# A selective-scan layer with its MLP on one core: accumulating DMAs chained over three states instead of two

## The chip, the core and the metric

The kernel runs on 1 core of a Trainium2 chip. The metric is the device time of one execution in microseconds (us). Engines are named as in the profile: PE is TensorE (PEld its weight loads), DVE is VectorE, ACT is ScalarE, POOL is GpSimd, SP is SyncE. "The clock" is the granted clock of TensorE, as a share of 2.4 GHz.

## What is computed

The input x has 4 batches of 4096 positions with 512 channels, all in float32. The layer is an adaptive layer norm, a selective scan with 16 states per channel, a gated output projection with residual and layer norm, and then a small per-channel MLP. Cut to what matters here:

```
h = layernorm(x) * (1 + ca) + sa
x_ssm, z = split(h @ w_in.T + b_in);  z = silu(z)
dt = softplus(x_ssm @ w_dt.T + b_dt)
Bm = x_ssm @ w_B.T + b_B;  Cm = x_ssm @ w_C.T + b_C
A = -exp(A_log)
def step(state, inp):                      # over the positions
    xt, dtt, bt, ct = inp
    dA = exp(A[None] * dtt[..., None])
    dB = dtt[..., None] * bt[:, None, :]
    state = dA * state + dB * xt[..., None]
    y = sum(state * ct[:, None, :], axis=-1)     # over the 16 states
y = (y + D * x_ssm) * z
x = x + ga * (layernorm(y @ w_out.T + b_out + h) * gamma + beta)
h = layernorm(x) * (1 + cb) + sb
x = x + gb * ffn(h)                        # 512 -> 64, relu of 16 each, -> 512
```

The change concerns the sum over the 16 states in the line that begins with `y = sum`.

## The kernel before

**Tiling.** The positions are cut into 32 chunks of 512, worked through one after another. In a chunk the channels stand on the partitions, in KD = 4 blocks of 128, and the scan runs along the 512 positions. A **unit** is one state of one channel block, so a chunk has 64 units: unit i is state i // 4, block i % 4. I call one pass over the 64 units a **step**, and position i in it **slot** i. In step s the scan of chunk s runs; beside it the dense work of the next chunk (norm, projections, dt, u: the tensors xs_t, dt_t, u_t) and of the two chunks before (output projection, second norm, MLP).

**One unit's way.** ACT makes the decay (L842) and, per state, the input v (L852). PE turns v into channel-major form in PSUM (`turn_v`, L524; the instruction's own line is L468, b_ps). The transpose for unit i + 1 stands at the start of slot i and waits until scan i - 1 is done. DVE scans (L1140, into `hs`, a ring of 6 units). POOL multiplies two units at once with C (L379, the product, into `pr`, a ring of 10 units). PE adds the product into y_ps by four transposes (`add_unit`, L533, instructions L543). Scan i needs product i - 6 to be done. A product needs its place in `pr` free: the unit ten before must have been added by PE, or copied on by a DMA.

**Chained states.** States in HELD are not added by PE. Once the next state's product is made, POOL issues a DMA (`add_products`, L387) that adds the held product into it, within SBUF: one DMA of 512 KB for two units. The sum of the two is added by PE. `summed(n)` says that state n receives such a sum. HELD = (0, 6, 8, 11), so states 1, 7, 9 and 12 receive: 8 DMAs and 48 adds in a step.

**Order.** Every engine has its own instruction order, made when the program is built. Each runs the loop over i and, after slot i's fixed work, whatever of its side chains is due (`Beside.until(i)`). POOL's fixed work is the product at odd i and the DMA issue after it. Its side chains that matter here: `attended` (L393: gs_shift added into x1, L399; then the x1 addition, L404, once for each of 4 row tiles, due from slot 13 to 24), `step_size` (L413: L417 adds into dt_t, L425 makes u_t, due in slots 42 to 52) and `gate` (L428). In slots SKIP_AT, POOL also adds D * x into the product (L385). DVE's second statistics (L1157 in `second_statistics`, on x1) are due at slots 19, 22, 25 and 26; they wait for the x1 addition of their tile. PE's `turn_u` (L697) waits for the last u_t. PE's adds are due in the slot that `add_slot` gives: four after the unit, seven after for a unit that receives a sum. `ADDS` is the list of the units that PE adds, in that order.

All these waits hold the whole queue: an instruction behind a waiting one on its engine waits too.

Of the kernel before, what the change touches and what calls it, by code (L numbers as in the profile page):

```python
def build_program(nc, ap, B, L, D, N, M, INNER):
# [11 lines left out]
    KD = D // P  # L13
# [5 lines left out]
    Q = 16  # L19
# [2 lines left out]
    V_RING, DEC_RING, HS_RING, PR_RING, C_RING = 2, 6, 6, 10, 3  # L22
    LAG = 4

    HELD = (0, 6, 8, 11)
    SUM_LAG = 3
    RELU_RING = 3


    SKIP_AT = (8, 10)  # L30

# [31 lines left out]
    def summed(n):  # L65
        return n - 1 in HELD

    def sums(i):

        return sum(summed(n) for n in range(i // KD + 1))  # L70

    def add_slot(r):

        return r + LAG + SUM_LAG * summed(r // KD) - (r in (U - 4, U - 2, U - 1)) - (r == U - 1)

    ADDS = sorted((r for r in range(U) if r // KD not in HELD), key=lambda r: (add_slot(r), r))

    def added(r):

        return ADDS.index(r) + 1  # L80
# [11 lines left out]
    with ctx:  # L92
# [80 lines left out]
        def inside(s, *group):  # L173
# [24 lines left out]
        S = {n: ctx.enter_context(nc.semaphore(n)) for n in once + list(COUNT)}  # L198
        x_loaded, xb_loaded, c_loaded, wm_loaded, sum_done = (
            [ctx.enter_context(nc.semaphore(f"{n}_{m}")) for m in range(count)]  # L200
            for n, count in (("x_loaded", TB), ("xb_loaded", TB), ("c_loaded", C_RING), ("wm_loaded", 6), ("sum_done", KD // 2)))

        def at(name, k, n):

            return (k + FIRST) * COUNT[name] + n if k < NCH else (NCH + FIRST) * COUNT[name]

        SUMS = Q * len(HELD)

# [140 lines left out]
        def _(gp):  # L349
# [13 lines left out]
            def both(ring, of, i):  # L363

                return ring[:, i % of:i % of + 2, :]

            def product(s, i):
# [5 lines left out]
                for q in (r, r + 1):  # L373
                    if q // KD not in HELD:
                        gp.wait_ge(S["y_added"], at("y_added", k, added(q)))
                if r // KD in HELD and k >= 0:
                    gp.wait_ge(sum_done[r % KD // 2], k * SUMS + Q * sums(r + KD))
# [3 lines left out]
                                 ).then_inc(S["prod_done"], 1)  # L381
                if i in SKIP_AT:
                    gp.wait_ge(S["prod_done"], at("prod_done", s, i // 2 + 1))
# [3 lines left out]
            def add_products(s, i):  # L387

                gp.wait_ge(S["prod_done"], at("prod_done", s, i // 2 + 1))
                gp.dma_start(both(pr, PR_RING, s * U + i), both(pr, PR_RING, s * U + i - KD), accum_op=ALU.add  # L390
                             ).then_inc(sum_done[i % KD // 2], Q)

# [48 lines left out]
            def step(s, has_s, has_f, has_b, has_c):  # L441
                f, b = s + 1, s - 1
                chains = []
                if has_b:
                    chains += [last_gate(b), attended(b)]
                if has_b and b % NC == 0:
                    chains.append(gate_out(b // NC))
                if has_f:
                    chains.append(step_size(f, b))
                if has_s:  # L450
                    chains.append(gates(s))
                beside = Beside(*chains)
                for i in range(U):
                    if has_s and i % 2:
                        product(s, i - 1)
                        if summed(i // KD):
                            add_products(s, i - 1)
                    beside.until(i)
# [4 lines left out]
        def _(pe):  # L463
# [69 lines left out]
            def add_unit(s, i):  # L533
# [5 lines left out]
                pe.wait_ge(S["prod_done"], at("prod_done", s, i // 2 + 1))  # L539
                if i - j % 2 in SKIP_AT:  # L540
                    pe.wait_ge(S["skip_added"], at("skip_added", s, j // 2 + 1))
# [790 lines left out]
```

## Time and profile before

| what | us |
|---|---|
| median of 3 runs | 4576.69 |
| lowest, highest | 4574.44, 4577.13 |
| profiled execution: its own time | 4574.68 |
| span of the profiled execution | 4572.9 |
| busy of PE, ACT, DVE, POOL | 4356.8, 3814.2, 3698.9, 3596.2 |
| idle before the products (L379), most of it for scans | 765.9 |
| DMA queue of POOL: share of 16 engines | 15.3% |
| DMA queue of SP: share of 16 engines | 17.4% |

The table is read so: no engine is idle for long, and PE has the least room. Busy shares over the whole span hide that the side chains fill different engines in different slots of a step, so the rows below go by stretches of one step. In a timeline row the first number is the start in us from the span's beginning, the second the duration; in square brackets stands how long the engine was idle before, and who ended it.

### The profile page before, as it was taken

To read this page: it belongs to the slowest core of one execution; us is meant where nothing else is said; L and a number is where in the kernel's file an instruction comes from. 1 tells how busy PE (TensorE), PEld (TensorE's weight loads), DVE (VectorE), ACT (ScalarE), POOL (GpSimd) and SP (SyncE) were. 2 spreads that over 40 slices of the span, in tenths; PEclk is the share of its full clock that TensorE was granted. 3 is DMA by queue.
4 is the path that set the end of the run, shared out by engine and by line. 5 is a ranking of instruction groups with operands and counts; after the bars stand their busy time and mean duration, and the time that the engine had idled before them with its cause. 6 is when DMAs were issued, how large, how long until landed. Compare 5 with 4: busy or idle time off the path is not lost. (4 is left out here: it accounts for less than half of the span.)

```text
span 4572.9 us, 69933 instructions
## 1 busy us (share of the span) xinstructions
PE 4356.8 (95%) x22528; PEld 2784.8 (61%) x22528; DVE 3698.9 (81%) x5132; ACT 3814.2 (83%) x6371; POOL 3596.2 (79%) x1999
## 2 busy tenths in 40 slices
PE   7999999999999999999999999999999999999997
PEld 3666666666666666666666666666666666666664
DVE  3778888888888888888888888888888888888885
ACT  3788888888888888888888888888888888888885
POOL 3787878887878877877878878878788878788784
PEclk8999999999999999999999999999999999999999
DMA  4233233333233333332333333332333333333322
GB/s 138 73 79 87 81 89 82 85 81 88 80 94 81 83 88 87 85 87 77 86 93 83 89 82 84 83 90 78 91 76 89 87 86 86 86 77 89 86 77 58
DMA packets 177763, 388.89 MB, mean 85 GB/s; under 512 B 22693, under 2 KB 22693, under 8 KB 177402
## 3 DMA queue, kind: packets, MB, share of 16 engines
q1 hardware_dynamic: 140538, 250.19, 17.4%
q0 software_dynamic: 36864, 134.23, 15.3%
q8 instruction: 184, 3.01, 0.3%
q14 instruction: 177, 1.45, 0.1%
HBM read 215.50 MB, written 34.63 MB: 55 GB/s over the span
## 5 line engine op out<-in xcount | busy, mean ns | idle before, releaser
L379 POOL TENSOR_TENSOR work<-work,c_bc 128x1024 f32<-128x1024 f32 x1024 | 2463.3, 2418 | 765.9 <-DVE work L1140 676.7
L1140 DVE TENSOR_TENSOR_SCAN work<-work,state,b_ps 128x512 f32<-128x512 f32 x1792 | 2257.7, 1274 | 301.1 <-PE b_ps L468 272.7
L852 ACT ACTIVATE work<-u_td,b_td 128x512 f32<-128x512 f32 x2048 | 1453.2, 710 | 163.7 <-PE b_ps L468 158.3
L842 ACT ACTIVATE work<-dt_t,neg_a 128x512 f32<-128x512 f32 x2048 | 1451.3, 709 | 4.7 <-DVE work L1140 4.4
L468 PE MATMUL b_ps<-ident,work 128*128 128x128 f32 x8192 | 1253.3, 276 | 65.0 <-DVE work L1140 57.1
L468 PEld LDWEIGHTS b_ps<-ident,work 128*128 128x128 f32 x8192 | 974.8, 142 | 505.3 <-issue 303.2
L543 PEld LDWEIGHTS y_ps<-ident,work 128*128 128x128 f32 x6144 | 740.0, 142 | 481.7 <-issue 466.0
L543 PE MATMUL y_ps<-ident,work 128*128 128x128 f32 x6144 | 862.8, 273 | 1.6 <-DMA work<-work 1.3
L692 PE MATMUL dense<-h_t,w_in_t 128*128 128x512 f32 x1024 | 514.5, 599 | 1.1 <-DVE u_td L1223 1.1
L600 PE MATMUL dense<-w_out_t,proj 128*128 128x512 f32 x1024 | 509.9, 595 | 0.0
L658 PE MATMUL dense<-xs_t,w_dt_t 128*128 128x512 f32 x1024 | 501.2, 593 | 0.0
L629 PE MATMUL dense<-h_t,w_in_t 128*128 128x512 f32 x1024 | 498.4, 595 | 1.0 <-ACT h_t L856 1.0
L1140 DVE TENSOR_TENSOR_SCAN work<-work,b_ps 128x512 f32<-128x512 f32 x256 | 307.4, 1213 | 61.5 <-PE b_ps L468 57.5
L468 PE MATMUL dense<-ident,xn 128*128 128x128 f32 x1536 | 243.6, 283 | 92.4 <-POOL xn L425 45.8
L468 PEld LDWEIGHTS dense<-ident,xn 128*128 128x128 f32 x1536 | 180.3, 144 | 226.9 <-issue 98.7
L390 POOL DMA_DIRECT2D work<-work x256 | 225.2, 880 | 81.9 <-POOL work L379 74.4
L552 PE MATMUL dense<-tmp,w_dg 128*128 128x512 f32 x512 | 245.3, 593 | 1.8 <-ACT tmp L874 1.8
L874 ACT ACTIVATE tmp<-gm,b,w 128x512 f32<-128x512 f32 x256 | 202.7, 804 | 49.4 <-PE dense L552 25.8
L692 PEld LDWEIGHTS dense<-h_t,w_in_t 128*128 128x128 f32 x1024 | 166.7, 190 | 104.1 <-issue 101.5
L629 PEld LDWEIGHTS dense<-h_t,w_in_t 128*128 128x128 f32 x1024 | 168.5, 191 | 82.9 <-issue 82.9
L417 POOL TENSOR_TENSOR dt_t<-dt_t,tmp 128x512 f32<-128x512 f32 x128 | 173.0, 1352 | 49.9 <-ACT tmp L984 49.9
L658 PEld LDWEIGHTS dense<-xs_t,w_dt_t 128*128 128x128 f32 x1024 | 165.5, 191 | 66.9 <-issue 66.9
(115 smaller groups left out, 4530.4 us busy)
## 6 DMA issues: line engine op xcount, KB each, us to landing
c_bc<-c_d SPq DMA_DIRECT2D x512, 256.0 KB, 3.3
work<-work POOLq DMA_DIRECT2D x256, 512.0 KB, 5.6
xn<-in_x SPq DMA_DIRECT2D x128, 256.0 KB, 5.1
x<-in_x SPq DMA_DIRECT2D x128, 256.0 KB, 4.3
out_dram<-x SPq DMA_DIRECT2D x128, 256.0 KB, 4.4
work<-in_wmod SPq DMA_DIRECT2D x2, 1024.0 KB, 6.5
w_in_t<-in_w_in_t SPq DMA_DIRECT2D x2, 1024.0 KB, 9.9
gain_shift<-par_d SPq DMA_DIRECT2D x8, 256.0 KB, 6.0
```

Source lines behind the costliest of these rows:

```text
L379: gp.tensor_tensor(made_here, both(hs, HS_RING, s * U + i), c_bc[:, (s * N + n) % C_RING:(s * N + n) % C_RING + 1, :].to_broadcast([P, 2, ...
L390: gp.dma_start(both(pr, PR_RING, s * U + i), both(pr, PR_RING, s * U + i - KD), accum_op=ALU.add).then_inc(sum_done[i % KD // 2], Q)
L468: return nc.tensor.transpose(dst, src, ident[:, :])
L543: last = mm(y_ps[:, tb, j * P:(j + 1) * P], pr[:, (s * U + i) % PR_RING, tb * P:(tb + 1) * P], ident[:, :], is_transpose=True, start=(i == ...
L552: mm(long(s, "g")[:, :], w2_dg[:, k, :], tmp[:, k % RELU_RING, :], start=(k == 0), stop=(k == J - 1)).then_inc(S["g_used"], 1)
L600: last = mm(long(s, "pre", tb)[:, :], yz_t[:, k, tb * P:(tb + 1) * P], w_out[:, k, :], start=False, stop=(k == KD - 1))
L629: last = mm(long(s, "xs", m)[:, :], w_in[:, k, m * P:(m + 1) * P], h_t[:, f % 2, k, :], start=(k == 0), stop=(k == KD - 1))
L658: last = mm(long(s, "dt", m)[:, :], w_dt[:, k, m * P:(m + 1) * P], xs_t[:, k, :], start=(k == 0), stop=(k == KD - 1))
L692: last = mm(long(s, "z", m)[:, :], w_in[:, k, D + m * P:D + (m + 1) * P], h_t[:, s % 2, k, :], start=(k == 0), stop=(k == KD - 1))
L842: A(decay[:, (s * U + i) % DEC_RING, :], dt_t[:, s % 2, j, :], ACT.Exp, scale=neg_a[:, j, n:n + 1]).then_inc(S["dec_done"], 1)
L852: A(v[:, n % V_RING, tb, :], u_td[:, tb, :], ACT.Copy, scale=b_td[:, s % 2, tb, n:n + 1]).then_inc(S["v_done"], 1)
L1140: V.tensor_tensor_scan(hs[:, (s * U + i) % HS_RING, :], decay[:, (s * U + i) % DEC_RING, :], b_ps[:, i % 2, :], state[:, i:i + 1] if s % N ...
```

## The change

HELD becomes (0, 1, 3, 4, 6, 7, 9, 10). States 0, 1, 2 form a chain, and 3, 4, 5, and 6, 7, 8, and 9, 10, 11; states 12 to 15 stay single. In a chain the first product is added into the second by a DMA, and the sum of both into the third by another, and only the third is added by PE. There are 16 DMAs and 32 adds in a step. The second DMA of a chain first waits on POOL until the first has landed. SKIP_AT moves the two skip additions from units 8 and 10 (state 2) to units 12 and 14 (state 3), and the DMA that reads such a product waits for them. All lines from 390 on are four further down in the kernel after.

```diff
-    HELD = (0, 6, 8, 11)
+    HELD = (0, 1, 3, 4, 6, 7, 9, 10)
-    SKIP_AT = (8, 10)
+    SKIP_AT = (12, 14)
@@ def add_products(s, i):
                 gp.wait_ge(S["prod_done"], at("prod_done", s, i // 2 + 1))
+                if i - KD in SKIP_AT:
+                    gp.wait_ge(S["skip_added"], at("skip_added", s, i % KD // 2 + 1))
+                if summed(i // KD - 1):
+                    gp.wait_ge(sum_done[i % KD // 2], s * SUMS + Q * sums(i - KD))
                 gp.dma_start(both(pr, PR_RING, s * U + i), both(pr, PR_RING, s * U + i - KD), accum_op=ALU.add
                              ).then_inc(sum_done[i % KD // 2], Q)
```

Where it moves instructions. First POOL from the product of units 18, 19 to the last x1 addition of a chunk. L379 is the product, L399 and L404 (L403 and L408 after) the two x1 operations. Before:

```order
L379 TENSOR_TENSOR work<-work,c_bc 128x1024 [waits y_added,scan_done]
L399 TENSOR_TENSOR x<-x,gain_shift 128x512 [waits xb_loaded_2]
L379 TENSOR_TENSOR work<-work,c_bc 128x1024 [waits y_added,scan_done,c_loaded_2]
L404 TENSOR_TENSOR x<-x,tmp 128x512 [waits t2_done,xsh_done]
L399 TENSOR_TENSOR x<-x,gain_shift 128x512 [waits xb_loaded_3]
L379 TENSOR_TENSOR work<-work,c_bc 128x1024 [waits y_added,scan_done]
L404 TENSOR_TENSOR x<-x,tmp 128x512 [waits t2_done,xsh_done]
```

POOL at the same place after:

```order
L379 TENSOR_TENSOR work<-work,c_bc 128x1024 [waits y_added,scan_done]
L394 DMA work<-work 128x1024 [waits skip_added,prod_done]
L403 TENSOR_TENSOR x<-x,gain_shift 128x512 [waits xb_loaded_2]
L379 TENSOR_TENSOR work<-work,c_bc 128x1024 [waits y_added,scan_done,c_loaded_2]
L394 DMA work<-work 128x1024 [waits sum_done_0,prod_done]
L408 TENSOR_TENSOR x<-x,tmp 128x512 [waits t2_done,xsh_done]
L403 TENSOR_TENSOR x<-x,gain_shift 128x512 [waits xb_loaded_3]
L379 TENSOR_TENSOR work<-work,c_bc 128x1024 [waits sum_done_0,scan_done]
L394 DMA work<-work 128x1024 [waits sum_done_1,prod_done]
L408 TENSOR_TENSOR x<-x,tmp 128x512 [waits t2_done,xsh_done]
```

Three DMA issues stand between that were not there; a fourth stands behind the product of units 16, 17, and a skip addition behind each of the two products before that.

Second, PE in slots 28 and 29. L468 b_ps (L472 after) is the transpose for the next unit, L629 (L633) a projection matmul, L543 (L547) a y add. Before:

```order
L468 MATMUL b_ps<-ident,work 128x128 [waits scan_done]
L468 MATMUL b_ps<-ident,work 128x128 x3
L629 MATMUL dense<-h_t,w_in_t 128x512 x2
```

After, from the transpose for unit 29 to that for unit 31:

```order
L472 MATMUL b_ps<-ident,work 128x128 [waits scan_done]
L472 MATMUL b_ps<-ident,work 128x128 x3
L633 MATMUL dense<-h_t,w_in_t 128x512 x2
L547 MATMUL y_ps<-ident,work 128x128 [waits prod_done,sum_done_0]
L547 MATMUL y_ps<-ident,work 128x128 x3
L472 MATMUL b_ps<-ident,work 128x128 [waits scan_done]
L472 MATMUL b_ps<-ident,work 128x128 x3
L633 MATMUL dense<-h_t,w_in_t 128x512
L547 MATMUL y_ps<-ident,work 128x128 [waits prod_done,sum_done_1]
L547 MATMUL y_ps<-ident,work 128x128 x3
L472 MATMUL b_ps<-ident,work 128x128 [waits scan_done]
```

Adds of chained sums (units 21 and 22) have come into slots that had no add; they wait for DMAs (sum_done).

Third, POOL from the product of units 44, 45 to the last u_t (L425, then L429). Before:

```order
L379 TENSOR_TENSOR work<-work,c_bc 128x1024 [waits sum_done_1,scan_done,c_loaded_2]
L417 TENSOR_TENSOR dt_t<-dt_t,tmp 128x512 [waits ldt_done]
L425 TENSOR_TENSOR xn<-dt_t,xs_t 128x512 [waits dt_done]
L379 TENSOR_TENSOR work<-work,c_bc 128x1024 [waits y_added,scan_done]
L417 TENSOR_TENSOR dt_t<-dt_t,tmp 128x512 [waits ldt_done]
L379 TENSOR_TENSOR work<-work,c_bc 128x1024 [waits y_added,scan_done,c_loaded_0]
L390 DMA work<-work 128x1024 [waits prod_done]
L425 TENSOR_TENSOR xn<-dt_t,xs_t 128x512 [waits dt_done]
L379 TENSOR_TENSOR work<-work,c_bc 128x1024 [waits y_added,scan_done]
L390 DMA work<-work 128x1024 [waits prod_done]
L417 TENSOR_TENSOR dt_t<-dt_t,tmp 128x512 [waits ldt_done]
L425 TENSOR_TENSOR xn<-dt_t,xs_t 128x512 [waits dt_done]
```

After:

```order
L379 TENSOR_TENSOR work<-work,c_bc 128x1024 [waits y_added,scan_done,c_loaded_2]
L394 DMA work<-work 128x1024 [waits sum_done_0,prod_done]
L421 TENSOR_TENSOR dt_t<-dt_t,tmp 128x512 [waits ldt_done]
L429 TENSOR_TENSOR xn<-dt_t,xs_t 128x512 [waits dt_done]
L379 TENSOR_TENSOR work<-work,c_bc 128x1024 [waits sum_done_0,scan_done]
L394 DMA work<-work 128x1024 [waits sum_done_1,prod_done]
L421 TENSOR_TENSOR dt_t<-dt_t,tmp 128x512 [waits ldt_done]
L379 TENSOR_TENSOR work<-work,c_bc 128x1024 [waits sum_done_1,scan_done,c_loaded_0]
L429 TENSOR_TENSOR xn<-dt_t,xs_t 128x512 [waits dt_done]
L379 TENSOR_TENSOR work<-work,c_bc 128x1024 [waits sum_done_0,scan_done]
L421 TENSOR_TENSOR dt_t<-dt_t,tmp 128x512 [waits ldt_done]
L429 TENSOR_TENSOR xn<-dt_t,xs_t 128x512 [waits dt_done]
```

The two issues have moved ahead, from units 48 and 50 to 44 and 46, and the products of units 40, 41 and 42, 43 before this piece have one each.

## Rows read from the trace of the kernel before

**Rows 1.** The page, busy time of each engine:

```profile
PE 4356.8 (95%) x22528; PEld 2784.8 (61%) x22528; DVE 3698.9 (81%) x5132; ACT 3814.2 (83%) x6371; POOL 3596.2 (79%) x1999
```

**Rows 2.** One line of code, L1164, once per step, 900 to 1330 us.

```profile
L1164 DVE COPY gm<-dense x4: 690/692/692, 907.7 to 1323.1; 128x512 f32<-128x512 f32 x4
```

**Rows 3.** Busy time in stretches of one step; (x) counts instructions.

```profile
2331.40:2363.90 32.50, 31.86 (x182) 21.90 (x181) 27.51 (x45) 26.80 (x49) 27.63 (x17) 1.00 0.30 89
...
2395.40:2420.30 24.90, 23.60 (x117) 13.71 (x116) 18.39 (x25) 19.79 (x35) 23.62 (x15) 1.00 0.32 78
2420.30:2439.80 19.50, 19.50 (x117) 13.98 (x116) 15.38 (x22) 14.92 (x25) 13.98 (x8) 1.00 0.25 83
```

The columns are the stretch, its length, busy time of PE, PEld, DVE, ACT, POOL, then the granted clock, the DMA engines' share and GB/s.

**Rows 4.** Timeline of PE, slots 27 to 29.

```profile
2364.46 0.60 PE L543 MATMUL y_ps<-ident,work 128*128 128x128 f32 x4
2364.89 0.60 PE L468 MATMUL b_ps<-ident,work 128*128 128x128 f32 x4
2365.33 1.88 PE L629 MATMUL dense<-h_t,w_in_t 128*128 128x512 f32 x4
2367.05 0.60 PE L468 MATMUL b_ps<-ident,work 128*128 128x128 f32 x4
```

**Rows 5.** POOL by line, busy and mean ns, idle before.

```profile
L390 POOL DMA_DIRECT2D work<-work x256 | 225.2, 880 | 81.9 <-POOL work L379 74.4 <-issue 7.5
```

**Rows 6.** Timeline of POOL, two DMA issues, from the first.

```profile
2370.11 0.88 POOL L390 DMA_DIRECT2D work<-work  x1 [0.30 <-POOL work L379]
2370.72 1.59 POOL L430 TENSOR_TENSOR sz_t<-sz_t,tmp 128x512 f32<-128x512 f32 x1
2371.95 2.68 POOL L379 TENSOR_TENSOR work<-work,c_bc 128x1024 f32<-128x1024 f32 x1
2374.93 0.88 POOL L390 DMA_DIRECT2D work<-work  x1 [0.30 <-POOL work L379]
2375.54 2.66 POOL L379 TENSOR_TENSOR work<-work,c_bc 128x1024 f32<-128x1024 f32 x1
```

**Rows 7.** Timeline of DVE: scans 13, 14; last statistics on x1; scan 27.

```profile
2330.26 2.53 DVE L1140 TENSOR_TENSOR_SCAN work<-work,b_ps 128x512 f32<-128x512 f32 x2
...
2361.58 0.68 DVE L1157 BATCH_NORM_STATS2 norm<-x 128x6 f32<-128x512 f32 x1
...
2362.47 1.22 DVE L1140 TENSOR_TENSOR_SCAN work<-work,b_ps 128x512 f32<-128x512 f32 x1
```

**Rows 8.** Timeline of POOL, products of units 12 to 15, x1 operations.

```profile
2332.53 2.36 POOL L379 TENSOR_TENSOR work<-work,c_bc 128x1024 f32<-128x1024 f32 x1
2337.48 2.37 POOL L379 TENSOR_TENSOR work<-work,c_bc 128x1024 f32<-128x1024 f32 x1 [2.59 <-DVE work L1140]
2339.81 1.27 POOL L399 TENSOR_TENSOR x<-x,gain_shift 128x512 f32<-128x512 f32 x1
...
2358.25 1.30 POOL L404 TENSOR_TENSOR x<-x,tmp 128x512 f32<-128x512 f32 x1
```

**Rows 9.** POOL by line: products and skip additions.

```profile
L379 POOL TENSOR_TENSOR work<-work,c_bc 128x1024 f32<-128x1024 f32 x1024 | 2463.3, 2418 | 765.9 <-DVE work L1140 676.7 <-issue 87.6 <-PE y_ps L543 0.5
...
L385 POOL TENSOR_TENSOR work<-work,xs_t 128x1024 f32<-128x1024 f32 x64 | 151.5, 2368 | 5.0
```

**Rows 10.** Timeline of POOL: products of units 42 and 48, last u_t.

```profile
2395.39 2.37 POOL L379 TENSOR_TENSOR work<-work,c_bc 128x1024 f32<-128x1024 f32 x1 [1.19 <-DVE work L1140]
...
2408.01 2.35 POOL L379 TENSOR_TENSOR work<-work,c_bc 128x1024 f32<-128x1024 f32 x1 [0.53 <-issue]
...
2417.72 1.27 POOL L425 TENSOR_TENSOR xn<-dt_t,xs_t 128x512 f32<-128x512 f32 x1
```

**Rows 11.** The accumulating DMAs, from issue to landing.

```profile
DMA to landing us min/median/max: 4.5/5.6/8.1
```

**Rows 12.** Waits of PE: us in total, times, longest.

```profile
PE dense L468 <- POOL xn L425: 45.8, 32, 2.8
```

## The prediction

> **What bounds the kernel now.** I read the busy times first, then a middle step by stretches, then each engine's timeline in it. TensorE (PE) is busy for 95% of the span, ScalarE 83%, VectorE (DVE) 81%, GpSimd (POOL) 79% [rows 1]. Steps in the middle are 138.5 us apart (415.4 us over three) [rows 2]; the one that I follow, from its scan 0 at 2301.9 to the next at 2439.8, is 137.9 us. In three stretches of it PE is busy 31.9 of 32.5, 23.6 of 24.9 and 19.5 of 19.5 us, at a granted clock of 1.00, the 2.4 GHz level [rows 3]. Matmul spans overlap, so I check with starts: a y add (four transposes, L543) begins at 2364.46 and the next group at 2364.89, and that one's successor at 2365.33 [rows 4]. No gap, and 0.435 us for each group of four. So PE sets the pace almost everywhere. But POOL is close behind, and not evenly: in the first stretch of rows 3 it is busy 27.6 of 32.5 us, in the second 23.6 of 24.9, in the third only 14.0 of 19.5. The change takes from the first engine and gives to the second.
>
> **A rule that speaks against a gain.** PE's weight loads fill only 21.9 of 32.5 us where its matmuls fill 31.9 [rows 3]. The Trainium skill ("Perfetto Trace Analysis", Identifying the Most-Contended Engine) says that matmul busy time is no good measure of PE's headroom, that the busy share of its weight loads is to be used, and that the engine with the highest occupancy is to be relieved first. By that rule PE is at 61% over the span and ScalarE leads, so the removed adds would bring nothing. The starts in rows 4 say otherwise: PE has no free time between groups. I keep the rule as rival 2.
>
> **Part 1: adds leave PE.** ADDS falls from 48 to 32 units, so 16 x 0.435 = 7.0 us of PE work go from each of 32 steps: 223 us in all. The cut is uneven. By the slots that add_slot gives, slots 11 to 27 go from 20 adds to 5, slots 28 to 50 from 12 to 7, and slots 51 to 65 from 16 to 20. This is a gain only where PE is still the last to finish.
>
> **Part 2: DMA issues come to POOL.** From 8 accumulating issues in a step to 16. Price of one: the issue waits 0.30 us for the product before it (always, the wait is for POOL's own result), and the next instruction starts 0.61 us after the issue's start (2370.11 to 2370.72), which makes 0.91. While the issue still runs (0.88 us), the follower is stretched: products that come after one take 2.65 us and not 2.37 [rows 5, 6], and so the next issue comes later. From product 2371.95 to the next at 2375.54 are 3.59 us against 2.35 without an issue: 1.2 us. I take 1.2, with 0.91 as lower end. Eight more are 9.6 us in a step on POOL, whose busy time is 3596 us in 32 steps, 112 a step [rows 1]: together 122, and waits for its own results come on top. That would still fit if it were spread evenly.
>
> **Part 3: where they land.** I give the product of units p, p+1 the name Pp. I follow four stretches.
>
> (a) From scan 13's end to the transpose for unit 29. Scan 13 is the first of the two that begin at 2330.26 and ends at 2331.5 [rows 7]. POOL before has P12 at 2332.53 and P14 at 2337.48 after 2.59 us of idleness, and ends the last x1 addition (L404) at 2358.25 + 1.30 = 2359.55 [rows 8]. VectorE asks for that x1 tile at slot 26, by the statistics at 2361.58; it was ready 2 us before. After the change the skip additions (L385, 2.37 us [rows 9]) stand behind P12 and P14 and no longer behind P8 and P10, and issues stand behind P16, P18, P20 and P22, where there was none. POOL's queue from P12 to the last x1 addition: six products x 2.35 = 14.1, two skips x 2.37 = 4.7, eight L399/L404 x 1.27 = 10.2, some 0.4 for waits for its own results, four issues x 1.2 = 4.8: 34.2 us. From 2331.5 this ends at 2365.7. VectorE's queue is in order: statistics at slot 26 wait for it, then 0.9 us (2361.58 to 2362.47), then scan 27 at 2366.6, which ended at 2363.7 before and now at 2367.8 [rows 7]. Unit 29's transpose waits for scan 27; it began at 2364.89 [rows 4] and now begins at about 2367.9: **+3.0 us**, though PE has lost 6 us of work there. The stretch grows from 33.4 to 36.4 us. Queued behind that wait on VectorE are scan 27 and all that follows, and behind them PE and POOL. With 0.91 per issue it is +1.8.
>
> (b) From there to P42 (2395.39, which waited 1.19 us for scan 43 [rows 10]) PE sets the pace before and after. Units 21, 22 and 23 are now added in slots 28 to 30 (3), units 32 to 34 in slots 39 to 41 (3), and units 28 to 31 no longer in 35 to 38 (-4): +2 x 0.435 = **+0.9 us**, 30.5 to 31.4. Are the chained sums there in time? DMAs land 4.5 to 8.1 us after issue, median 5.6 [rows 11]. The last issue of (a), for P22, is at 2363.5 and lands at 2369.2; PE comes to unit 22 at 2367.9 + 0.4 + 1.7 + 0.4 + 0.4 + 0.9 = 2371.7. It is covered by 2.5 us, and if the landing took 8.1 us PE would just not wait.
>
> (c) From P42 to the end of the last L425 (2417.72 + 1.27 = 2419.0 [rows 10]). PE turns that tensor and waits for POOL there in every step: 45.8 us in 32 waits, 1.4 each [rows 12]. So this chain is already on the path. Before it held two issues (behind P48 and P50) and 0.5 us of idleness; now three (P42, P44, P46): 23.6 + 1.2 - 0.5 = 24.3, **+0.7 us**. What PE saves in slots 43 to 53 (three adds net) only makes its wait longer.
>
> (d) From there to the next step's scan 13: 50.4 us. PE has no gap here [rows 3]. One add fewer in slots 54 to 63 gives **-0.4**; the one that leaves slot 11 lies where VectorE is full, and I count nothing.
>
> Sum: +3.0 + 0.9 + 0.7 - 0.4 = +4.2, and I round to **+4 us a step**. (a) needs a step that also finishes an earlier chunk, and (c) one that prepares a later one, so 31 steps, rounded: 31 x 4 = 124 us. The profiled execution took 4574.7 us around a span of 4572.9, so it comes to 4699; the median of the three runs is 4576.7, 2 us higher, which gives 4701. I say **4700**.
>
> **Bounds.** The low price of an issue (0.91) takes 1.2 from (a) and 0.3 from (c): 2.7 us a step (4.2 - 1.5), 4660. If P12 or P14 come a microsecond earlier or some waits of PE overlap with the new delay, 1 to 2 us a step: 4608 to 4640. Upward: sixteen DMAs of 512 KB share the queues with the c_bc and x transfers, and landings of 8.1 us and some waits at unit 22 would add 1 to 2 us: 4730 to 4763. Below nothing is open only through the rivals.
>
> **Rivals.**
> 1. PE stays the bound: 7.0 us a step go, 4576.7 - 223 = 4354, faster. For it speaks PE's 95%. Its place is slots 11 to 27; it decides the time if POOL's queue from P12 to the last x1 addition takes less than about 30 us rather than 34.2. Against it: the rows that the 34.2 is made of hold no idleness but 2.59 us. If half of it came true, 4465.
> 2. No change, 4577: the issues fall into POOL's idle time (2.59 us before P14, 1.19 before P42 [rows 8, 10]) and PE's savings pay for the rest. It needs +0 and not +3 in (a). The rule of the Trainium skill quoted above would come to the same time, by another way: PE was never the bound.
> 3. The DMAs become the bound. The chain needs one landing before the next issue. If landings grew past 8 us, PE waits at units 22 and 34 and POOL at its issues, 3 us more each step: 4700 + 93 = 4793. Against it: the issues of one chain are over 8 us apart, and the DMA engines are busy for 0.30, 0.32 and 0.25 of the three stretches [rows 3].
> 4. That the change doesn't do what it says: the order of instructions shows sixteen issues and 32 adds a step, so I give it nothing.
>
> **How the numbers follow.** The forecast gets 0.70, rival 1 with its half case 0.11, rival 2 0.12, rival 3 0.07. The range runs from 4560 (rival 2, a little better than no change) to 4765 (upper bound), and leaves out rival 1, most of rival 3 and little else. What a measurement can tell from no change is 0.2%, 9 us. Faster: rival 1 and a quarter of rival 2 = 0.14. Same: half of rival 2 and a little of the forecast's lower end = 0.08. Slower: 0.78.
>
> **What would show it.** PE's busy time falls by some 220 us while the span grows; PE's busy share comes down to about 88%. POOL's idleness before L379, 766 us before [rows 9], falls to some 570. VectorE shows a new wait, of its statistics on x1 (L1161 by then) for POOL's L408, of 3 to 4 us once a step. PE's wait for the last L429 grows from 1.4 to about 2.5 us a step. Unit 22's add shows no wait for a DMA, or a short one. The steps are about 142.5 us apart. I'm wrong in (a) if that VectorE wait is missing, in the price if POOL's product after an issue is not stretched, and in (b) if PE waits there for anything but scans.

## The result: 4.6% slower, and the profile after

| | us |
|---|---|
| before, median (range) of 4 | 4576.42 (4574.44 to 4577.13) |
| after, median (range) of 4 | 4786.31 (4785.0 to 4789.25) |
| ratio after / before, 95% interval | 1.0461 (1.0448 to 1.0475) |
| span of the profiled execution | 4784.1 |
| forecast, range | 4700, 4560 to 4765 |

The direction was forecast and the place too, but the loss is 210 us and not 124, and the time lies above the range. A part of it came from something that the forecast had taken as constant, TensorE's clock.

The page of after, busy times and the groups that answer to [rows 1, 5, 9] (columns as there):

```profile
PE 4266.3 (89%) x20480; PEld 2596.5 (54%) x20480; DVE 3737.9 (78%) x5132; ACT 3819.5 (80%) x6371; POOL 3827.1 (80%) x2255
...
L379 POOL TENSOR_TENSOR work<-work,c_bc 128x1024 f32<-128x1024 f32 x1024 | 2502.2, 2446 | 668.2 <-DVE work L1144 530.7
...
L394 POOL DMA_DIRECT2D work<-work x512 | 449.3, 877 | 163.9 <-POOL work L379 148.9
L633 PE MATMUL dense<-h_t,w_in_t 128*128 128x512 f32 x1024 | 542.6, 642 | 8.5 <-ACT h_t L860 8.5
...
L1161 DVE BATCH_NORM_STATS2 norm<-x 128x6 f32<-128x512 f32 x128 | 88.5, 691 | 192.5 <-POOL x L408 192.5
```

Three things stand here. PE is busy for only 90 us less, though 2048 transposes are gone that took 223 us from start to start. The matmuls of L633 have 642 ns each; the same ones (L629) had 595 before. And VectorE's statistics on x1 wait 192.5 us for POOL's L408, a wait that was not among those before.

Who waits for whom (us in total, times, longest) shows the second link of the chain, from VectorE to PE: PE waits for scans, 57.1 us before, 314.7 now.

```profile
DVE norm L1161 <- POOL x L408: 192.5, 93, 4.5
...
PE b_ps L472 <- DVE work L1144: 314.7, 249, 6.1
PE dense L472 <- POOL xn L429: 58.4, 32, 2.8
```

**One step, at the place of stretch (a).** The step starts at 2111.1 (its first scan); its scan 13 ends at 2141.2. POOL's timeline from the product of units 12, 13:

```profile
2141.42 2.35 POOL L379 TENSOR_TENSOR work<-work,c_bc 128x1024 f32<-128x1024 f32 x1 [0.43 <-issue]
2143.86 2.35 POOL L385 TENSOR_TENSOR work<-work,xs_t 128x1024 f32<-128x1024 f32 x1
2147.50 2.38 POOL L379 TENSOR_TENSOR work<-work,c_bc 128x1024 f32<-128x1024 f32 x1 [1.29 <-DVE work L1144]
...
2157.53 0.88 POOL L394 DMA_DIRECT2D work<-work  x1 [0.30 <-POOL work L379]
2158.14 1.58 POOL L403 TENSOR_TENSOR x<-x,gain_shift 128x512 f32<-128x512 f32 x1
...
2174.47 0.88 POOL L394 DMA_DIRECT2D work<-work  x1 [0.30 <-POOL work L379]
2175.08 1.56 POOL L408 TENSOR_TENSOR x<-x,tmp 128x512 f32<-128x512 f32 x1
```

The last x1 addition ends at 2175.08 + 1.56 = 2176.6. VectorE meanwhile:

```profile
2170.68 0.69 DVE L1161 BATCH_NORM_STATS2 norm<-x 128x6 f32<-128x512 f32 x1 [1.96 <-POOL x L408]
...
2176.68 0.69 DVE L1161 BATCH_NORM_STATS2 norm<-x 128x6 f32<-128x512 f32 x1 [3.76 <-POOL x L408]
2177.40 0.18 DVE L1163 BATCH_NORM_AGGREGATE norm<-norm 128x2 f32<-128x6 f32 x1
2177.58 2.45 DVE L1144 TENSOR_TENSOR_SCAN work<-work,state,b_ps 128x512 f32<-128x512 f32 x2
```

These are the waits for the third tile at slot 25 and for the last at slot 26; for the first, at slot 19, it waited 0.43 us. That makes the 93 waits of the page, three in a step. Scan 27 begins at 2177.58. And PE, the timeline that answers to [rows 4]:

```profile
2174.34 0.60 PE L547 MATMUL y_ps<-ident,work 128*128 128x128 f32 x4
2178.92 1.12 PE L472 MATMUL b_ps<-ident,work 128*128 128x128 f32 x4 [3.98 <-DVE work L1144]
2179.83 3.62 PE L633 MATMUL dense<-h_t,w_in_t 128*128 128x512 f32 x4
2183.24 0.90 PE L547 MATMUL y_ps<-ident,work 128*128 128x128 f32 x4
2183.98 0.60 PE L472 MATMUL b_ps<-ident,work 128*128 128x128 f32 x4
2184.42 1.02 PE L633 MATMUL dense<-h_t,w_in_t 128*128 128x512 f32 x2
```

After a pause of 4 us (3.98 in brackets) the group of four transposes takes 0.91 us from start to start, not 0.435, and the four projection instructions 3.41 us, not 1.72. From 2183.98 on all is as before. The same stretches by engine, then the granted clock (columns as in [rows 3]):

```profile
2144.30:2178.92 34.62, 25.67 (x123) 14.94 (x121) 26.66 (x39) 25.53 (x46) 31.90 (x20) 0.97 0.57 139
2178.92:2187.42 8.50, 8.50 (x29) 5.11 (x30) 5.88 (x7) 6.21 (x11) 6.85 (x5) 0.71 0.25 54
```

In the 8.5 us after the pause the clock averages 0.71: for more than half of the time it was at 1.2 GHz. Before the change it was 1.00 in all the stretches shown [rows 3]. The Trainium skill ("TensorE: Matmul & The Clock Gate", What's actually happening) says that the clock is passed at half rate or in full by how busy the array has been of late, and this trace agrees: 0.71 after the pause, at the full level once PE had worked again.

The trace also says how regular this is. In each of the 28 steps of the table below the clock is at 1.2 GHz for a while around this pause, 5.1 us on average. In the 14 steps in which it is low for longer, the way from scan 27 to scan 31 takes 8.9 to 9.4 us, in the other 14 it takes 7.7 to 8.1; before it took 6.5. The step that I show is one of the two of the 28 in which the clock falls a second time, behind PE's wait for the last u_t, and that costs 2.4 us more (48.4 us from scan 43 to the next step and not 46.0).

**The loss by stretches.** Averages over 28 middle steps (all but the first two, the last two) of the starts of scans in VectorE's timeline, in us from scan 0. The lines below after are the experiments that follow:

| kernel | scan 13 | 27 | 31 | 43 | next scan 0 |
|---|---|---|---|---|---|
| before | 28.9 | 61.2 | 67.7 | 92.8 | 138.7 |
| after | 28.9 | 66.5 | 75.0 | 99.4 | 145.5 |
| e1_fill | 28.9 | 66.5 | 73.1 | 97.9 | 144.0 |
| e2_no345 | 28.9 | 61.9 | 68.4 | 93.2 | 139.4 |
| e3_skip8 | 28.9 | 64.7 | 72.6 | 97.0 | 143.1 |
| e4_skip_only | 28.9 | 61.6 | 68.0 | 93.2 | 139.2 |
| e5_late_stats | 28.9 | 61.7 | 72.4 | 96.8 | 142.9 |
| e6_only345 | 28.9 | 63.8 | 72.0 | 96.8 | 142.8 |
| e7_alt_0167 | 29.3 | 62.3 | 68.9 | 92.5 | 138.6 |
| e8_alt_0678 | 29.3 | 61.6 | 68.2 | 91.8 | 137.9 |
| e9_before_fill | 28.9 | 61.2 | 72.0 | 96.4 | 142.3 |
| e10_only345_fill | 28.9 | 63.8 | 70.7 | 95.5 | 141.5 |

Of the 6.8 us a step, 5.3 arise before scan 27, 2.0 between scans 27 and 31 (8.5 against 6.5), -0.8 from there to scan 43, and +0.3 in the rest. 31 steps of 6.8 us are 211 us, which is the whole difference (210).

### The profile page after: what moved, and what is told of

Its sections match the earlier page's. It is cut to its first block and busy times, and to the rows that moved or that the text cites. A ratio compares the mean times of both kernels' runs of the same rounds, so it can differ in the third digit from the quotient of the medians.

```text
span 4784.1 us, 66157 instructions
## 1 busy us (share of the span) xinstructions
PE 4266.3 (89%) x20480; PEld 2596.5 (54%) x20480; DVE 3737.9 (78%) x5132; ACT 3819.5 (80%) x6371; POOL 3827.1 (80%) x2255
## 3 DMA queue, kind: packets, MB, share of 16 engines
q0 software_dynamic: 73728, 268.47, 29.2%
## 5 line engine op out<-in xcount | busy, mean ns | idle before, releaser
L379 POOL TENSOR_TENSOR work<-work,c_bc 128x1024 f32<-128x1024 f32 x1024 | 2502.2, 2446 | 668.2 <-DVE work L1144 530.7
L472 PE MATMUL b_ps<-ident,work 128*128 128x128 f32 x8192 | 1280.5, 280 | 321.1 <-DVE work L1144 314.7
L472 PEld LDWEIGHTS b_ps<-ident,work 128*128 128x128 f32 x8192 | 985.9, 144 | 941.8 <-issue 503.8
L547 PEld LDWEIGHTS y_ps<-ident,work 128*128 128x128 f32 x4096 | 505.9, 144 | 367.1 <-issue 344.7
L547 PE MATMUL y_ps<-ident,work 128*128 128x128 f32 x4096 | 595.6, 276 | 3.8 <-DMA work<-work 3.2
L394 POOL DMA_DIRECT2D work<-work x512 | 449.3, 877 | 163.9 <-POOL work L379 148.9
L633 PE MATMUL dense<-h_t,w_in_t 128*128 128x512 f32 x1024 | 542.6, 642 | 8.5 <-ACT h_t L860 8.5
L696 PE MATMUL dense<-h_t,w_in_t 128*128 128x512 f32 x1024 | 517.4, 602 | 1.1 <-DVE u_td L1227 1.1
L472 PE MATMUL dense<-ident,xn 128*128 128x128 f32 x1536 | 244.7, 284 | 122.1 <-POOL xn L429 58.4
L472 PEld LDWEIGHTS dense<-ident,xn 128*128 128x128 f32 x1536 | 182.5, 144 | 252.2 <-issue 80.8
L633 PEld LDWEIGHTS dense<-h_t,w_in_t 128*128 128x128 f32 x1024 | 183.9, 208 | 112.2 <-issue 112.2
L421 POOL TENSOR_TENSOR dt_t<-dt_t,tmp 128x512 f32<-128x512 f32 x128 | 199.5, 1558 | 52.7 <-ACT tmp L988 52.7
L1161 DVE BATCH_NORM_STATS2 norm<-x 128x6 f32<-128x512 f32 x128 | 88.5, 691 | 192.5 <-POOL x L408 192.5
L993 ACT ACTIVATE tmp<-tmp 128x512 f32<-128x512 f32 x128 | 80.0, 625 | 196.3 <-DVE tmp L1242 196.3
```

The source lines that it names most:

```text
L379: gp.tensor_tensor(made_here, both(hs, HS_RING, s * U + i), c_bc[:, (s * N + n) % C_RING:(s * N + n) % C_RING + 1, :].to_broadcast([P, 2, ...
L472: return nc.tensor.transpose(dst, src, ident[:, :])
L547: last = mm(y_ps[:, tb, j * P:(j + 1) * P], pr[:, (s * U + i) % PR_RING, tb * P:(tb + 1) * P], ident[:, :], is_transpose=True, start=(i == ...
L633: last = mm(long(s, "xs", m)[:, :], w_in[:, k, m * P:(m + 1) * P], h_t[:, f % 2, k, :], start=(k == 0), stop=(k == KD - 1))
L696: last = mm(long(s, "z", m)[:, :], w_in[:, k, D + m * P:D + (m + 1) * P], h_t[:, s % 2, k, :], start=(k == 0), stop=(k == KD - 1))
```

## The experiments

My theory after the result: (1) POOL's queue up to the last x1 addition holds VectorE at slots 25 and 26, 5.3 us; (2) the pause that PE makes for it lowers its clock, 2.0 us up to scan 31. The rivals: twice as much DMA traffic, or POOL's higher load in general, slows everything; and, for the second term, something else after scan 27 is slow.

### e1_fill: work in PE's pause

```diff
+    FILL = 5
...
+                    if has_s and has_f and has_b and i == 27:
+                        for _ in range(FILL):
+                            mm(long(s, "xs", 1)[:, :], w_in[:, 0, 0:P], h_t[:, f % 2, 0, :], start=True, stop=True)
```

These stand in PE's loop behind the adds of slot 27; the bank is begun anew by the next projection group.

> The kernel after, with five matmuls more on TensorE in every full step, at the end of slot 27, into a PSUM bank that is overwritten by the next group; they need nothing that is late and stand just where TensorE then pauses for scan 27. Clock theory: the pause of 4 to 6 us is filled with 4.3 us of work, the granted clock stays at 1.00 afterwards, and the 2.5 to 3 us that TensorE lost at the 1.2 GHz level in each step come back: 4786 - 31 x 2.5 to 3.3 = about 4685 to 4710, with more TensorE work than before. Rival (the clock dips cost nothing, since TensorE waits anyway): 4786, or more if the extra 4.3 us don't fit into the pause.

Measured: 4737.96 us (4736.73 to 4741.19), 1.0357 of before (1.0342 to 1.0373), so 48 us faster than after, with 133 us of PE work more. Steps are 144.0 us apart. Between scans 27 and 31 the whole 2.0 us are back (6.5 us, as before); from there to scan 43 it takes 24.8 us where after took 24.3, so 1.5 us a step are gained in the end. PE in one step of it:

```profile
2155.41 0.60 PE L548 MATMUL y_ps<-ident,work 128*128 128x128 f32 x4
2155.85 4.46 PE L831 MATMUL dense<-h_t,w_in_t 128*128 128x512 f32 x10
2160.14 0.60 PE L473 MATMUL b_ps<-ident,work 128*128 128x128 f32 x4
2160.58 1.88 PE L634 MATMUL dense<-h_t,w_in_t 128*128 128x512 f32 x4
2162.30 0.60 PE L548 MATMUL y_ps<-ident,work 128*128 128x128 f32 x4
```

The second line is the added matmuls (five, shown as ten instructions). The group of four transposes takes 0.44 us again, and the clock is low around scan 27 in none of the 28 steps, where in the kernel after it was in all. The theory asked for 2.5 to 3.3 us a step; it was 1.5. So the mechanism is shown, and it is smaller than I read off one step. The rival falls.

### e9_before_fill: the same matmuls where there is no pause

The same edit in the kernel before.

> Control for the filled pause: the kernel before with the same five matmuls more at the end of slot 27. There TensorE has no pause for scan 27, so 5 x 0.86 = 4.3 us a step should come on top: 4577 + 31 x 4.3 = 4710, less what the step's other engines have to spare there (TensorE could be up to 2 us ahead again later): 4640 to 4710. Rival (these matmuls cost little anywhere, so the filled kernel says nothing of the pause): 4577 to 4600.

Measured: 4681.65 us, 1.0231 (1.0214 to 1.0248): 105 us slower, 3.4 us a step. So these matmuls aren't cheap; that they made the kernel after faster is then the clock's doing.

### e2_no345: the chain over states 3, 4, 5 taken out

```diff
-    HELD = (0, 1, 3, 4, 6, 7, 9, 10)
+    HELD = (0, 1, 6, 7, 9, 10)
```

> The kernel after without the chain over states 3, 4, 5: those are single, so the four DMA issues behind the products of units 16 to 22 are gone, and 8 adds are back on TensorE (40 in a step). 12 DMAs a step stay. Theory (the loss lies in POOL's queue from the product of unit 12 to the last x1 addition): the queue is 4.8 us shorter, VectorE's wait on x1 nearly goes, TensorE doesn't pause and its clock stays high: 4786 - 31 x (5 + 3) + little = 4530 to 4590. Rival (DMA traffic or POOL's total load slows the step evenly): half of the added DMAs are gone, so half of the loss: 4680.

Measured: 4595.12 us, 1.0045 (1.003 to 1.006). Four of the sixteen issues go, and 191 of the 210 us with them; VectorE's statistics wait 1.7 us in all for POOL, scan 27 is at 61.9, and the clock is low around it in no step. The rival of even slowing by DMA traffic or load would have given 4680. The place counts, not the number.

### e6_only345: that chain alone, in the kernel before

```diff
-    HELD = (0, 6, 8, 11)
+    HELD = (0, 3, 4, 6, 8, 11)
```

The four lines of waits in `add_products` are there too.

> The kernel before with one chain added: states 3, 4, 5 (four issues behind the products of units 16 to 22; 40 adds in a step, 12 DMAs), skip additions at 8 and 10 as before. This is the other half of what the run without that chain took out. Theory: POOL's queue to the last x1 addition gets 4.8 us longer against about 2 us to spare, so VectorE waits some 2 to 3 us a step, and the eight removed adds, in slots 16 to 23, bring nothing: 4577 + 31 x 2 to 3 = 4640 to 4670. Rival (eight adds fewer is a gain of 3.5 us a step, partly eaten): 4520 to 4577.

Measured: 4698.15 us, 1.0269 (1.0253 to 1.0284), 31 x 4 us, though 8 adds a step (3.5 us of PE) are gone. Its waits:

```profile
PE b_ps L472 <- DVE work L1144: 189.5, 147, 5.0
...
DVE norm L1161 <- POOL x L408: 118.2, 34, 5.1
```

Scan 27 is 2.6 us late, as expected, and 1.6 us come between scans 27 and 31; the clock is low around it in 22 of the 28 steps. The range that I gave, 4640 to 4670, left this second term out. On the price of an issue: from the product of unit 16 to that of unit 24, with four issues between, POOL takes 21.5 us where it took 17.1 before, so 1.1 us each.

### e10_only345_fill: its pause filled

The two edits of e6 and e1 together.

> The kernel before with the chain over states 3, 4, 5 (4698) and the five matmuls in slot 27. Clock theory: of its loss of 4 us a step 1.7 lie between scans 27 and 31 and are the lower clock after the pause: 4698 - 31 x 1.7 = 4645, with a granted clock near 1.00 there; the pause of some 4 us is about as long as the extra work, so up to 20 us may be lost again: 4645 to 4665. Rival (the stretch after scan 27 is slow for another reason, such as landings of DMAs): 4698 or more.

Measured: 4661.4 us, 1.0187 (1.0171 to 1.0202): 37 us faster than e6. Over 1000 to 4000 us of both kernels (columns as in [rows 3]), e6 first:

```profile
1000.00:4000.00 3000.00, 2786.93 (x14022) 1750.48 (x14020) 2412.93 (x3336) 2503.38 (x4175) 2431.50 (x1389) 0.98 0.40 97
```

```profile
1000.00:4000.00 3000.00, 2863.75 (x14384) 1787.85 (x14383) 2438.09 (x3365) 2527.70 (x4224) 2456.26 (x1403) 1.00 0.41 98
```

The clock is 1.00 instead of 0.98, and low around scan 27 in no step. From scan 27 to 31 it takes 6.9 us and not 8.2. A second kernel shows the clock's term.

### e4_skip_only: only the skip additions moved

```diff
-    SKIP_AT = (8, 10)
+    SKIP_AT = (12, 14)
```

> The kernel before with only the skip additions moved from units 8, 10 to 12, 14. Theory: POOL's queue from unit 12 to the last x1 addition becomes 4.7 us longer, but starts 1 us earlier and had 2.6 us of idleness and 2 us to spare at the end, so nothing waits: 4577, at most 4590. Rival (the moved skip additions alone make the loss of some 5 us a step): 4730.

Measured: 4590.05 us, 1.0031 (1.0018 to 1.0043). The move alone costs 0.5 us a step (15 us), a little more than the "nothing" of the theory. With the chain it costs more, which the next one shows.

### e3_skip8: the skip additions back in the kernel after

```diff
-    SKIP_AT = (12, 14)
+    SKIP_AT = (8, 10)
@@ def add_products(s, i):
+                if i in SKIP_AT:
+                    gp.wait_ge(S["skip_added"], at("skip_added", s, i % KD // 2 + 1))
```

> The kernel after with the two skip additions back behind units 8 and 10 (the DMA into such a product waits for its skip addition). POOL's total work and the DMAs are the same. Theory: 4.7 us leave the queue behind unit 12, but the start of that queue comes about 2 us later, so the wait on x1 falls by 2 to 3 us a step, the pause of TensorE with it, and perhaps the clock stays: 4786 - 31 x 2.5 = 4708, down to 4620 if the clock stays up. Rival (total load or DMA traffic): 4786.

Measured: 4710.11 us, 1.0296 (1.0281 to 1.0311). POOL does the same work and as many DMAs run, and 76 us are gone: 2.4 us a step, of which 1.8 are at scan 27. Together with e4: the moved skip additions cost 0.5 us where POOL has room, and 2.4 where it has none.

### e5_late_stats: VectorE asks two slots later

```diff
-    SECOND = [made("pre", tb, 3) + (5 if tb == TB - 1 else 9 - tb) for tb in range(TB)]
+    SECOND = [made("pre", tb, 3) + (7 if tb == TB - 1 else 9 - tb) for tb in range(TB)]
```

> The kernel after with VectorE's statistics on the last x1 tile two slots later (slot 28, not 26); nothing else is changed. Theory (VectorE's queue is held at slot 26 by the x1 addition, and the pause of TensorE and its lower clock follow from that): scans 27 and 28 go before the wait, so the transposes for units 29 and 30 and their projection matmuls are done while VectorE waits, the pause gets shorter, and most of the 5.3 + 2.1 us a step come back as far as the ring of six scans allows: 4786 - 31 x 4 to 6 = 4600 to 4660. Rival (POOL's queue itself is the limit, by the ring of scan results, whoever waits first): scan 28 is held by the product of unit 22 about 4 us later than before, so 4720 to 4780.

Measured: 4703.58 us, 1.0279 (1.0264 to 1.0294), 83 us faster than after, in neither range. Scan 27 starts at 61.7, 4.8 us earlier, but at scan 31 only 2.6 us of it are left. What came in its place:

```profile
DVE norm L1161 <- POOL x L408: 111.8, 93, 3.2
...
PE y_ps L547 <- DMA work<-work: 51.8, 32, 3.5
```

VectorE still waits 3.6 us a step, for the third tile at slot 25 as before (1.98 us in one step) and for the last now at slot 28 (1.15). PE waits 1.6 us a step for the landing of a DMA at a y add; the kernel after had 3.2 us of that wait in all. The clock is not what is left: PE's longest pause there is 1.4 us, and the clock is low in only 3 of the 28 steps. In PE's timeline (a step that starts at 2076.65) it is the third add after scan 27, so unit 22's:

```profile
2143.39 1.02 PE L633 MATMUL dense<-h_t,w_in_t 128*128 128x512 f32 x2
2145.67 0.66 PE L547 MATMUL y_ps<-ident,work 128*128 128x128 f32 x4 [1.26 <-DMA work<-work]
```

So both theories hold in part: the wait on x1 was the first in line, and right behind it stands POOL's queue again, by the sum that it delivers late.

### e7_alt_0167 and e8_alt_0678: chains where POOL has room

```diff
-    HELD = (0, 1, 3, 4, 6, 7, 9, 10)
+    HELD = (0, 1, 6, 7, 8, 12)
```

> The kernel after with HELD = (0, 1, 6, 7, 8, 12): chains 0-1-2, 6-7-8-9 and 12-13, skip additions at 12 and 14; 40 adds, 12 DMAs, no issue between units 12 and 27 nor between 40 and 51. Theory (adds count only where TensorE is the last, in slots 28 to 65; issues only in POOL's two crowded stretches): four adds fewer in slots 28 to 42, the u_t chain 2.4 us shorter, four adds fewer in slots 54 to 63, the moved skips cost 0.5: about -2.6 us a step, 4577 - 80 = 4495. Rival (any DMA beyond eight in a step costs more than its adds): 4600, as in the run without states 3, 4, 5, which has as many DMAs and adds.

```diff
-    HELD = (0, 1, 3, 4, 6, 7, 9, 10)
+    HELD = (0, 6, 7, 8, 12)
-    SKIP_AT = (12, 14)
+    SKIP_AT = (8, 10)
```

> As the previous, but HELD = (0, 6, 7, 8, 12) and skip additions at 8 and 10: 44 adds, 10 DMAs. The four adds that come back (state 1) stand in slots 11 to 14, where by the theory they cost nothing, and the skips are as before: -3.1 us a step, 4480, not slower than the previous. Rival (fewer adds are faster wherever they stand): slower than the previous by 4 x 0.435 us a step, 54 us.

Measured: e7 4571.7 us, 0.9992 (0.9982 to 1.0001), no change; e8 4553.48 us, 0.9952 (0.9935 to 0.9968), so faster than the kernel before by a half per cent. e8 has four adds more than e7, in slots 11 to 14, and two DMAs fewer, and its skip additions stand at 8 and 10; it is 18 us faster, about what e4 gives for the skip additions alone (15 us). So adds in that part of the step cost nothing that shows. But both gained less than expected (-0.1 and -0.8 us a step, not -2.6 and -3.1). From scan 31 to 43 e7 saves 1.5 us, about the four adds that I had counted (1.7). From scan 43 to the next step it saves nothing (46.1 us, before 45.9), where the rest of what I had expected, 1.4 us, should have come from. Four adds more stand in slots 43 to 53, which would explain why the two issues that left the u_t chain don't pay; I didn't test that part by itself.

## Why the prediction was wrong

**The direction and the place were right.** Rows of after show the wait of L1161 for L408; PE's work left slots 11 to 27 without a gain; the landings are as before (median 5.5 us, [rows 11] 5.6) and PE waits for them 3.2 us in all. Rival 1 and rival 2 fell. Rival 3 gave the nearest time, 4793, by the wrong mechanism. e2 and e6, which take the four issues out or put them in alone, settle the place. Not all the signs that the forecast named came out as stated: VectorE's new wait is 6.2 us a step in three pieces, the last of them 3.8, where one of 3 to 4 was named; PE's busy time fell by 90 us and not 220; POOL's idleness before L379 fell to 668 and not 570.

**The term that was missing.** Part 3 (b) and (d) have "PE sets the pace" at the price of [rows 4], 0.435 us for four transposes. That price holds at the 2.4 GHz level. The forecast itself had PE wait in (a), and it priced only the wait and put the cost of the matmuls behind it at nothing extra; after it the groups took 0.91 us until the clock was back. Measured: scan 31 is late by a further 2.0 us a step for it, and 1.5 of these are still there in the next step (the gain of e1), 48 us in all. The upper bound of the range, 4765, had no such term either; with it the result would have been inside.

**The term that was too small.** (a) was to move scan 27 from 2362.47 to 2366.6, by 4.1 us; it moved by 5.3. I let POOL's queue run from the end of scan 13 to the last x1 addition without a stop, 34.2 us. In the step above it takes 2176.6 - 2141.2 = 35.4 us, with a stop of 1.29 before the second product. Before there were 2.59 in the same place [rows 8], and I took them as gone since the queue was longer and PE had less to do. That is the step that failed: the product of units 14, 15 still needs scan 15, which VectorE started no earlier (35.0 us after scan 0, before 34.7), so that the first skip addition filled time in which POOL would have waited anyway, and 1.29 us of stop came on top of the 34.2. The prices themselves hold: 1.1 to 1.2 us for an issue, 2.4 for a skip addition.

**What was right in size.** The forecast had scan 27 late by 4.1 us and scan 43 by 3.9 (3.0 at unit 29's transpose, and 0.9), a change of -0.2 between them. In e1, where the clock's term is gone, it takes 31.4 us from scan 27 to scan 43 against 31.7 before (unrounded starts): -0.3. (c) and (d) were to add 0.3 and added 0.3. PE's wait for the last u_t was to grow from 1.4 to 2.5 us and is 58.4 / 32 = 1.8.

**The sum.** 4.2 forecast before rounding, 1.2 for (a), 1.5 for the clock, -0.1 for the rest of (b): 6.8, which is what was measured. Two effects are mixed in the -0.8 between scans 31 and 43: 0.3 are the adds of (b), which e1 shows as well, and 0.5 are time lost to the clock that is made good there. What makes it good I haven't traced.

## What to carry to other kernels

When work is moved from the busiest engine to another, ask at each place of the loop which queue the receiving engine must deliver to, and by when; here 4 of 8 new DMA issues, 1.1 us each, stood in front of what VectorE asks for at fixed slots. Alone they cost 123 of the 210 us (e6), two skip additions moved into the same queue cost 15 us alone and 76 on top of the issues (e4, e3), and without the four issues nine tenths of the loss were gone (e2). Such terms don't add up singly, since the first of them only uses up the room that there was. A pause of TensorE is dearer than its length: price the matmuls after it at the 1.2 GHz level as well, and see whether the pause can be filled or spread. And work that leaves an engine that is 95% busy brings nothing in a stretch where another one becomes the last: 15 of PE's adds went from slots 11 to 27 for nothing.

## What the runs showed of the hardware

A pause of 4 us on TensorE, once in a step of 145 us, came with a clock of 1.2 GHz in all of 28 steps: 0.71 granted over the 8.5 us behind it, transposes at 0.91 us for four and not 0.435. With the pause filled it happened in none. The clock also fell elsewhere without such a pause, about 26 us after scan 0 in 8 of the 28 steps of after and in 10 of e1, where PE's pauses are 0.8 and 1.0 us; scan 27 started no later for it. More work on the same engine made a kernel faster, by 48 us in one and 37 us in another, where the same work cost 105 us in a kernel without the pause. Twice as many accumulating DMAs of 512 KB, at 29.2% of the 16 engines' time and not 15.3%, landed as fast as before (median 5.5 us, before 5.6).
